# Summing attention messages by node: building the one-hot matrices on GpSimd and ScalarE, storing messages in one piece per partition, and four product buffers

## The reference, cut to what matters

```python
ex = jnp.exp(a - amax[dst])
den = jax.ops.segment_sum(ex, dst, num_segments=n)
alpha = ex / (den[dst] + 1e-16)
...
h = jnp.concatenate([hs, hv.reshape(e, H, AV * 3)], axis=-1)
agg = jax.ops.segment_sum(alpha * h, dst, num_segments=n)
agg_s = agg[:, :, :AS_].reshape(n, H * AS_)
agg_v = agg[:, :, AS_:].reshape(n, H * AV, 3)
out = node + jnp.concatenate([agg_s @ Wps, jnp.einsum('ncx,cd->ndx', agg_v, Wpv).reshape(n, CV * 3)], axis=-1)
```

## Time and profile before

| | us |
|---|---|
| median of 3 runs | 6368.14 (6365.52 to 6386.07) |
| the profiled execution | 6384.29 |
| its span in the profile | 6382.5 |
| the attention pass, first to last store of messages | 2451.3 to 4608.8 |
| the message sums, first one-hot matrix to last window addition | 4739.2 to 5069.8 |

### The profile page before, as it was taken

The page is one execution under the profiler, slowest core; times in us unless marked ns, Lnnn a source line. Parts: engine busy times, 40 slices in busy tenths (PEclk is TensorE's granted clock), DMA queues, the critical chain, the costliest instruction groups (busy, mean ns, idle before and its releaser), DMA issues. The chain is left out here.

```text
span 6382.5 us, 222418 instructions
## 1 busy us (share of the span) xinstructions
PE 5592.3 (88%) x76769; PEld 4395.9 (69%) x76769; DVE 4128.0 (65%) x11379; ACT 2435.8 (38%) x6601; POOL 4074.9 (64%) x4031
## 2 busy tenths in 40 slices
PE   5898898788788859999999999999838879999998
PEld 3666666566666648888888888888727634777776
DVE  5566666345555547888888888888658775444443
ACT  3222222112222226777777777777600012111111
POOL 2777777577777746777777777777400012777776
PEclk9999999898888868999999999999869956999999
DMA  2444444455554533333333333333327502555554
GB/s 78 125 139 136 135 138 135 107 138 134 132 131 132 135 90 81 94 97 95 95 97 95 95 97 94 95 97 94 88 78 198 147 8 62 144 140 140 140 140 117
DMA packets 735477, 720.04 MB, mean 113 GB/s; under 512 B 249274, under 2 KB 594602, under 8 KB 734674
## 3 DMA queue, kind: packets, MB, share of 16 engines
q1 hardware_dynamic: 547154, 396.46, 21.8%
q0 software_dynamic: 188160, 321.38, 20.2%
HBM read 557.61 MB, written 159.75 MB: 112 GB/s over the span
## 5 line engine op out<-in xcount | busy, mean ns | idle before, releaser
L892 POOL DMA_INDIRECT l_edge_g<-node_table,l_edge_idx x2352 | 2249.0, 956 | 1003.3 <-issue 671.1
L938 PE MATMUL l_edge_win_ps<-l_edge_hot,l_edge_prod 128*32 128x40 f32 (+1 forms) x47040 | 1217.2, 227 | 300.8 <-issue 193.5
L938 PEld LDWEIGHTS l_edge_win_ps<-l_edge_hot,l_edge_prod 128*32 128x32 f32 x47040 | 1147.2, 116 | 462.6 <-issue 413.9
L966 ACT ACTIVATE l_edge_h<-l_edge_h_ps 128x256 f32<-128x256 f32 (+1 forms) x784 | 342.7, 437 | 2321.9 <-PE l_edge_h_ps L913 2098.2
L1002 DVE TENSOR_TENSOR l_edge_prod<-l_edge_w_ps,l_edge_g 128x512 f32<-128x512 f32 x588 | 406.1, 691 | 1216.4 <-DMA l_edge_g<-node_table,l_edge_idx 950.5
L1887 POOL DMA_INDIRECT att_g<-node_table,att_ends x784 | 896.6, 1144 | 286.1 <-issue 245.6
L1889 POOL DMA_INDIRECT att_g_dst<-node_table,att_ends x784 | 795.5, 1015 | 239.7 <-issue 239.7
L1909 PE MATMUL att_turn<-ident,sums_T 128*128 128x128 f32 (+1 forms) x4704 | 696.2, 284 | 38.0 <-ACT sums_T L1997 30.1
L1997 ACT ACTIVATE sums_T<-att_turn 128x512 f32<-128x512 f32 (+1 forms) x1176 | 662.8, 595 | 119.3 <-PE att_turn L1909 112.8
L920 PEld LDWEIGHTS l_edge_w_ps<-l_edge_wo,l_edge_h 64*128 64x128 f32 (+1 forms) x4704 | 501.3, 189 | 286.6 <-issue 244.1
L920 PE MATMUL l_edge_w_ps<-l_edge_wo,l_edge_h 64*128 64x192 f32 (+1 forms) x4704 | 676.8, 349 | 0.0
(11 more groups left out here) (281 smaller groups left out, 9319.8 us busy)
## 6 DMA issues: line engine op xcount, KB each, us to landing
l_edge_hot<-hot_tiles SPq DMA_DIRECT2D x392, 320.0 KB
hot_tiles<-l_edge_hot SPq DMA_DIRECT2D x196, 320.0 KB
l_messages<-att_rows SPq DMA_DIRECT2D x196, 320.0 KB, 2.8
sum_msg<-l_messages SPq DMA_DIRECT2D x196, 320.0 KB, 3.5
l_edge_g<-node_table,l_edge_idx POOLq DMA_INDIRECT x2352
att_g<-node_table,att_ends POOLq DMA_INDIRECT x784
att_ea<-in_edge_attr_T SPq DMA_DIRECT2D x196, 64.0 KB
att_g_dst<-node_table,att_ends POOLq DMA_INDIRECT x784
```

The lines of the kernel that those rows point to most:

```text
L892: pool.indirect_dma_start(g[s][:, t, :], None, rows_of, bass.IndirectOffsetOnAxis(idx[s][:, t:t + 1], 0)).then_inc(fetched[s], 16)
L938: return nc.tensor.matmul(win[n * VC:(n + 1) * VC, block * W:(block + kinds) * W], q[:, t, lo:lo + VC], to[:, t, kind:kind + kinds, :], st ...
```

## The change

The loop of `gather_messages` is spread over four engines, and the layout of `messages` in DRAM changes.

- POOL computes `away` = `iota_win` - `dst_rel` (four buffers) instead of DVE's comparison.
- ACT takes the absolute value of `away` in place, and in the next step makes `hot` = relu(1 - |away|), which is 1 where the numbers agree and 0 elsewhere, since they are whole numbers. ACT also makes the copy of the weights into `prod`.
- DVE keeps the product of messages and weights, and the window addition.
- `prod` and `hot` have four buffers each; `win_ps` still has two.
- In DRAM each partition's four message rows (2560 bytes) stand in one piece, both when stored and when loaded; before, they were four rows of 640 bytes apart.

```diff
-    messages = nc.dram_tensor("l2_messages", (EPAD, FEAT), F32).ap()
+    messages = nc.dram_tensor("l2_messages", (NG * P, TG * FEAT), F32).ap()
...
-                                sp.dma_start(messages[ds(k * GE, GE), :].rearrange("(t p) f -> p t f", p=P),
-                                             rows[(s + 1) % U][:, :, :, :].rearrange("p t h f -> p t (h f)")).then_inc(stored[(s + 1) % U], 16)
+                                sp.dma_start(messages[ds(k * P, P), :], rows[(s + 1) % U][:, :, :, :].rearrange("p t h f -> p (t h f)")
+                                             ).then_inc(stored[(s + 1) % U], 16)
...
-                prod = [sbuf(ctx, f"{tag}sum_prod{s}", [P, TG, 2, BW]) for s in range(2)]
-                hot = [sbuf(ctx, f"{tag}sum_hot{s}", [P, TG, SUM_WIN]) for s in range(2)]
+                prod = [sbuf(ctx, f"{tag}sum_prod{s}", [P, TG, 2, BW]) for s in range(U)]
+                away = [sbuf(ctx, f"{tag}sum_away{s}", [P, TG, SUM_WIN]) for s in range(U)]
+                hot = [sbuf(ctx, f"{tag}sum_hot{s}", [P, TG, SUM_WIN]) for s in range(U)]
+                unit = sbuf(ctx, f"{tag}sum_unit", [P, 1])
...
                     def _(pool):
+                        nc.gpsimd.memset(unit[:, :], 1.0).then_inc(unit_made, 1)
...
+                        pool.wait_ge(placed, 2)
+
+                        def step(i, s, r):
+                            at_least(pool, hot_made, i - 3)
+                            nc.gpsimd.tensor_tensor(away[s][:, :, :], iota_win[:, :].unsqueeze(1).to_broadcast([P, TG, SUM_WIN]),
+                                                    dst_rel[:, ds(i * TG, TG)].unsqueeze(2).to_broadcast([P, TG, SUM_WIN]),
+                                                    ALU.subtract).then_inc(away_made, 1)
+
+                        steps(pool, NG, 0, step, warm=8, unroll=U)
...
-                                s1 = (s - 1) % 2
-                                at_least(pe, made, i * K)
+                                s1 = (s - 1) % U
+                                at_least(pe, shares_put, i)
+                                at_least(pe, hot_made, i)
+                                at_least(pe, made, i)
                                 at_least(pe, added, i - 2)
...
+                        def step(i, s, r):
+                            if live(i, NG):
+                                at_least(act, away_made, i + 1)
+                                nc.scalar.activation(away[s][:, :, :], away[s][:, :, :], ACT.Abs).then_inc(unsigned, 1)
+                                at_least(act, summed, i - 3)
+                                e = exps[:, ds(i * TG * HEADS, TG * HEADS)].rearrange("p (t h) -> p t h", h=HEADS)
+                                nc.scalar.activation(prod[s][:, :, :, 2 * HF:BW], e.unsqueeze(2).to_broadcast([P, TG, 2, HEADS]), ACT.Copy
+                                                     ).then_inc(shares_put, 1)
+                            if live(i - 1, NG):
+                                s1 = (s - 1) % U
+                                at_least(act, summed, i - 4)
+                                at_least(act, unsigned, i)
+                                nc.scalar.activation(hot[s1][:, :, :], away[s1][:, :, :], ACT.Relu, scale=-1.0, bias=unit[:, :]
+                                                     ).then_inc(hot_made, 1)
...
                         def products(i, s, r):
-                            at_least(dve, made, i * K)
-                            at_least(dve, summed, i - 1)
-                            nc.vector.tensor_tensor(hot[s % 2][:, :, :], iota_win[:, :].unsqueeze(1).to_broadcast([P, TG, SUM_WIN]),
-                                                    dst_rel[:, ds(i * TG, TG)].unsqueeze(2).to_broadcast([P, TG, SUM_WIN]),
-                                                    ALU.is_equal).then_inc(made, 1)
+                            at_least(dve, summed, i - 3)
                             at_least(dve, msg_loaded[s], 16 * (r + 1))
...
-                            nc.vector.tensor_copy(prod[s % 2][:, :, :, 2 * HF:BW], e.unsqueeze(2).to_broadcast([P, TG, 2, HEADS])).then_inc(made, 1)
```

More of the change, by code:

```diff
@@ L2321, in gather_messages @@
             BW = 2 * HF + HEADS
-            K = 3
             U = 4
@@ L2333, in gather_messages @@
                 msg_loaded = [sem(ctx, f"{tag}sum_msg_loaded{s}") for s in range(U)]
+                unit_made = sem(ctx, f"{tag}sum_unit_made")
+                away_made = sem(ctx, f"{tag}sum_away_made")
+                unsigned = sem(ctx, f"{tag}sum_unsigned")
+                hot_made = sem(ctx, f"{tag}sum_hot_made")
+                shares_put = sem(ctx, f"{tag}sum_shares_put")
                 made = sem(ctx, f"{tag}sum_made")
@@ L2342, in step @@
                         def step(i, s, r):
-                            at_least(sp, made, (i - 3) * K)
-                            sp.dma_start(msg[s][:, :, :], messages[ds(i * GE, GE), :].rearrange("(t p) f -> p t f", p=P)
-                                         ).then_inc(msg_loaded[s], 16)
+                            at_least(sp, made, i - 3)
+                            sp.dma_start(msg[s][:, :, :].rearrange("p t f -> p (t f)"), messages[ds(i * P, P), :]).then_inc(msg_loaded[s], 16)
                         steps(sp, NG, 0, step, unroll=U)
@@ L2369, in step @@
                                     for t in range(TG):
-                                        ins = nc.tensor.matmul(win_ps[s1][0:BW, b * SUM_WIN:(b + 1) * SUM_WIN], prod[s1][:, t, b, :],
+                                        ins = nc.tensor.matmul(win_ps[s1 % 2][0:BW, b * SUM_WIN:(b + 1) * SUM_WIN], prod[s1][:, t, b, :],
                                                                hot[s1][:, t, :], start=t == 0, stop=t == TG - 1)
@@ L2378, in _ @@
                         act.wait_ge(zeroed, 2)
+                        act.wait_ge(unit_made, 1)
+                        def step(i, s, r):
[12 more added lines that the diff above has]
+                                                     ).then_inc(hot_made, 1)
+                        steps(act, NG, 1, step, warm=8, unroll=U)
                     @block.vector
@@ L2385, in products @@
                         def products(i, s, r):
-                            at_least(dve, made, i * K)
-                            at_least(dve, summed, i - 1)
-                            nc.vector.tensor_tensor(hot[s % 2][:, :, :], iota_win[:, :].unsqueeze(1).to_broadcast([P, TG, SUM_WIN]),
-                                                    dst_rel[:, ds(i * TG, TG)].unsqueeze(2).to_broadcast([P, TG, SUM_WIN]),
-                                                    ALU.is_equal).then_inc(made, 1)
+                            at_least(dve, summed, i - 3)
                             at_least(dve, msg_loaded[s], 16 * (r + 1))
                             e = exps[:, ds(i * TG * HEADS, TG * HEADS)].rearrange("p (k h) -> p k h", h=2)
-                            nc.vector.tensor_tensor(prod[s % 2][:, :, :, 0:2 * HF].rearrange("p t b (h f) -> p (t b) h f", h=2),
+                            nc.vector.tensor_tensor(prod[s][:, :, :, 0:2 * HF].rearrange("p t b (h f) -> p (t b) h f", h=2),
                                                     msg[s][:, :, :].rearrange("p t (b h f) -> p (t b) h f", b=2, h=2),
                                                     e.unsqueeze(3).to_broadcast([P, 2 * TG, 2, HF]), ALU.mult).then_inc(made, 1)
-                            e = exps[:, ds(i * TG * HEADS, TG * HEADS)].rearrange("p (t h) -> p t h", h=HEADS)
-                            nc.vector.tensor_copy(prod[s % 2][:, :, :, 2 * HF:BW], e.unsqueeze(2).to_broadcast([P, TG, 2, HEADS])).then_inc(made, 1)
                         def step(i, s, r):
```

## The result

The changed kernel takes 6308.86 us, median of 4 runs (6306.88 to 6315.08), against 6367.54 of the kernel before (4 runs, 6365.52 to 6386.07): a ratio of 0.9903, 95% interval 0.9883 to 0.9923. It is 58.7 us faster. The prediction was 6312, 56 us faster. Its number held; the reason for it did not, as the experiments show.

What follows compares the result with a forecast made beforehand. It took turns of DVE and POOL at SBUF to bound the message sums, 0.70 + 0.55 + 0.10 = 1.35 us a group. 196 x (1.647 - 1.35) less 1.8 gave 56.4 us saved, 6312 us, range 6278 to 6408.

Steps and rivals of the forecast that it cites:

- The loop of two buffers: Message sums: DVE and PE wait for each other over two buffers, 1.53 us becoming 1.65 a group; four buffers remove it.
- DVE 1.19 us a group: DVE in the message sums keeps product 0.74, addition 0.37 and 0.08 between: 1.19 us a group.
- uncovered 0.5: DVE's register work for a window, 0.305 load and 0.19 register piece: costed at nothing behind the product, 0.5 us if uncovered.
- Turns of DVE and POOL 1.35 us, the bound: DVE's product and POOL's subtraction take turns reading SBUF: 0.70 + 0.55 + 0.10 = 1.35 us a group, ends 1.08 and 1.50.
- POOL's hold of 0.55: Time POOL's subtraction holds SBUF in each group, as long as its reads: middle of 0.44 to 0.66 us.
- PE 1.2: PE's sixteen weight loads in the message sums: some 1.2 us a group when it never waits.
- ACT at most 1.12, hidden: ACT's three activations in the message sums: at most 1.12 us a group, below the other engines, costing nothing.
- Layout 0: Larger message pieces: loads fit and are hidden; the store's effect on the attention pass taken as 0, bounds -19.5 and +19.5 us.
- Start +1.8 us: Start of the message sums: first one-hot matrix needs two subtractions and two activations, about 3.2 us against 1.36, +1.8 once.
- A: Rival for the message sums: no turns that matter; DVE, PE and DMA bound, 1.22 us a group, 6286 us; chance 0.12.
- B: Rival: POOL holds its port for its whole instruction, DVE its whole recorded time; 1.84 to 2.06 a group, 6429; chance 0.15.
- C: Rival between: POOL's hold adds 0.40 us, 1.54 to 1.65 a group; 6359 us, no change that can be told; chance 0.17.

Runs made afterwards that it cites:

- buffers_only: The kernel before with four buffers of `prod` and `hot` and DVE's wait loosened to match, nothing moved off DVE: 6350.0 us, ratio 0.9967.
- fixed_window: The changed kernel with every window added at the same fixed columns, so DVE needs no register for the place (sums wrong): ratio 0.9938 to before.
- old_layout: The changed kernel with message rows stored and loaded as before, in pieces of 640 bytes: ratio 0.9909 to the kernel before.
- four_banks: The changed kernel with four PSUM banks `win_ps` in place of two: ratio 0.9938 to the kernel before on the same chip.

## Why the prediction was right in its number and wrong in its reason

- **The loop of two buffers: right, with half of its sign misread.** It was there and is gone; `buffers_only` prices it at 0.094 us a group. But of DVE's 97 waits for PE about half, 0.34 us each, stand at the turn of its loop, as in `buffers_only`. The distances between the products of the kernel before, 1.605, 1.665, 1.524 and 1.800 us, had shown the turn already.
- **DVE 1.19 us a group: near for a step, short for the loop.** The three steps without a turn of the loop take 1.203, 1.292 and 1.156, 1.217 on average. The prediction took its distances from one step and put the queue's register work at nothing because the product covers it. This is the step that failed. The product covers the register work as far as the engine goes, but the queue does one thing after another: load, register pieces, waits, the dispatch of the addition, waits, the dispatch of the product. That string is 1.15 to 1.29 us long by itself, whatever the engine does meanwhile, and the turn of the loop adds 0.46 us to every fourth. The forecast had no term for the turn at all, which is 0.11 us a group; nor would its "uncovered 0.5" have been right, since 1.19 + 0.5 is far from 1.32.
- **Turns of DVE and POOL 1.35 us, the bound: wrong as the bound, and too long.** The turns exist, as the earlier trace rows suggested: product 825 to 898 ns, subtraction 604 to 772. The forecast's own sign, a product of 1.0 to 1.3 us on average, was not met. POOL's hold of 0.55 was nearly right (0.57). DVE's hold was put at 0.70 and is 0.58 to 0.60; the 0.1 for hand-overs is not there. 1.15 to 1.17 replaces 1.35, and it lies under PE's 1.20 and the queue's 1.32. The estimate that followed from the Trainium skill (GPSIMD Engine Reference, "Elementwise — side-by-side cycle accounting"), 0.555 us for the elements, is near the 0.571 measured. The rule of a lock for the whole instruction (the Trainium skill, SBUF — State Buffer, "SBUF: two separate sides") does not hold here for DVE's side: 0.82 + 0.60 recorded would be 1.42 us a pair, and pairs came every 1.15.
- **So 1.35 met 1.32 by coincidence.** One term was 0.18 to 0.20 too long and another, the queue, was missing.
- **PE 1.2: right**, reached in `fixed_window`. **ACT at most 1.12, hidden: right**, the number by luck: its terms were 0.42, 0.42 and 0.28, and 0.496, 0.400 and 0.228 were measured. **Layout 0: right** for both the stage and the attention pass. Message loads land in 3.3 us (3.6 with the old layout), and in the changed kernel nobody waits for them.
- **Start +1.8 us: near.** The first weight load comes 2.95 us behind the first difference (4723.22 to 4726.17), where it took 1.36, so +1.6. The first rows of that start:

```profile
4723.22 5.78 POOL L2366 TENSOR_TENSOR sum_away<-iota_win,dst_rel 128x256 f32<-128x256 f32 x7
...
4726.20 3.03 PE L2387 MATMUL sum_win_ps<-sum_hot,sum_prod 128*84 128x64 f32 x20 [14.41 <-ACT sum_hot L2410]
```

- **The sum.** 196 x (1.649 - 1.321) = 64.3 us, of which the stage shows 60.8 (330.2 - 269.4) after its start and end, and the medians 58.7; predicted were 56.4.
- **The rivals.** A (no turns that matter, 1.22 a group) had the right view of POOL and missed DVE's queue by 0.10 us. B and C needed a POOL hold of 0.84 and more; it is 0.57.

Of the 1.32, nothing is PE showing through: DVE's distances are constant, and they stay the same with POOL idle, with four banks and with PE at half its clock. What is not settled is what some of the string's parts are made of. In the step of 1.292 us, 0.270 pass between the queue's last entry and the product, in the others 0.140 to 0.146, and no record stands in between; the 0.28 us behind the branch have no record either.

## What to carry to other kernels

Add up an engine's queue as a string of its own, from the start of one instruction to the start of the next: register loads, waits, dispatches and the loop's turn, which is spread over the groups that the loop is written out for. When the engine gets less to do, that string is what is left, and covering it with a long instruction does not shorten it. Idle time that a view puts down to another engine may be the queue's own turn: see whether the distance between its entries grows in front of the wait. A forecast that meets its number is not shown right by that; here one run with POOL out of the loop was enough to take its reason away.

## What the runs showed of the hardware that was not expected

- A window's register on DVE costs 0.30 us for the load and 0.19 for one register piece, and starting from the product 0.74 us pass before its queue is through with them. The turn of the loop has a recorded branch of 56 ns, but 0.28 us from its start to the next entry.
- DVE's product with two SBUF inputs, 820 ns recorded, keeps POOL's subtraction off for 0.58 to 0.60 us. The subtraction (256 elements a partition, two SBUF inputs) is recorded with 604 ns alone and starts every 0.571.
- The same kernel takes 6368 us on one chip and 10467 or 10636 on others. The idle time of POOL ahead of its gathers grows by 1.7 ms in the edge stages and by 1.5 ms in the attention pass, while the edge gathers keep their own 0.95 us, and the mean granted clock is 0.68 to 0.69 where it was 0.92. Which of the two comes first was not tested. The first line is from `old_layout` on the first chip, the second from `four_banks`:

```profile
L892 POOL DMA_INDIRECT l_edge_g<-node_table,l_edge_idx x2352 | 2264.7, 963 | 1003.7 <-issue 670.1 <-DMA l_edge_idx<-in_src_groups 281.8 <-DVE l_edge_prod L1006 18.0
```

```profile
L892 POOL DMA_INDIRECT l_edge_g<-node_table,l_edge_idx x2352 | 2244.3, 954 | 2701.8 <-issue 1801.4 <-DMA l_edge_idx<-in_src_groups 653.5 <-DVE l_edge_prod L1006 197.5
```

- With half the matmuls in the loop TensorE was granted 0.50 in this stage, in both runs, where it had 1.00 with all of them on the same chip (`four_banks`), so PE was busy 161 of 170 us. Half the work did not free the engine.
